# The second layout of an inner weight made by a transpose of the updated first one, and a gate's bias added by VectorE instead of by products

## What is computed

```python
def _recon(params, z):
    W1, b1, W2, b2 = params
    h = jax.nn.gelu(z @ W1.T + b1, approximate=False)
    return z + h @ W2.T + b2
def step(params, x):
    z, y = x @ t_k.T, x @ t_v.T
    grads = jax.grad(loss_fn)(params, z, y)      # mean squared error of _recon(params, z) against y
    new_params = tree_map(lambda p, g: p - LR * g, params, grads)
    return new_params, _recon(new_params, x @ t_q.T)
_, outs = jax.lax.scan(step, (W1, b1, W2, b2), in_seq)
```

```python
h2 = _rmsnorm(x, ffn_norm_w)
glogits = h2 @ gate_w + gate_b                   # 32 experts
topv, topi = jax.lax.top_k(glogits, 4)
gw = jax.nn.softmax(topv)
y2 = sum over the chosen experts e of gw_e * ((silu(g) * u) @ W_down[e]),  u, g = halves of h2 @ W_up[e]
```

## Time and profile before

| | |
|---|---|
| median of 3 runs | 968.82 us (968.16 to 969.98) |
| profiled execution | 970.77 us, of which the span of the core's instructions is 968.7 us |
| TensorE matmul busy | 849.8 us (88%), weight loads 649.2 us (67%) |
| VectorE, ScalarE, GpSimd busy | 762.2 us (79%), 593.1 us (61%), 478.4 us (49%) |
| mean granted TensorE clock | 0.943 of full |
| `layers` | to about 740 us; `experts` from there to the end |

### The profile page before, as it was taken

How to read it: one execution, slowest core, us unless ns; L and a number is a source line. 1 busy time by engine, 2 the same in 40 slices (tenths; PEclk the granted TensorE clock), 3 DMA queues, 4 the chain that set the end, 5 groups by cost and what they waited for, 6 DMA issues and landing times. The chain is left out here.

```text
span 968.7 us, 21670 instructions
## 1 busy us (share of the span) xinstructions
PE 849.8 (88%) x6666; PEld 649.2 (67%) x6666; DVE 762.2 (79%) x2734; ACT 593.1 (61%) x1900; POOL 478.4 (49%) x609
## 2 busy tenths in 40 slices
PE   1788999999999999999999999999984699999700
PEld 0445677777777777777777777777762588888600
DVE  2647979889898898989989898888865477777618
ACT  0114877768777786877868777687771366564300
POOL 1213223545555455555455555457436267777740
PEclk7699999999999999999999999999996799999955
DMA  6879999999940000000000000000001454444149
GB/s 160 261 241 374 375 374 375 370 371 366 364 109 20 8 19 17 11 21 11 19 10 17 18 14 20 7 19 26 19 16 39 110 142 125 132 128 112 53 134 334
DMA packets 97346, 129.41 MB, mean 134 GB/s; under 512 B 14513, under 2 KB 54354, under 8 KB 97234
## 3 DMA queue, kind: packets, MB, share of 16 engines
q1 hardware_dynamic: 84690, 108.36, 33.9%
q0 software_dynamic: 8192, 17.58, 5.5%
q10 hardware_dynamic: 4352, 2.10, 0.7%
HBM read 30.34 MB, written 97.65 MB: 132 GB/s over the span
## 5 line engine op out<-in xcount | busy, mean ns | idle before, releaser
L1322 POOL TENSOR_TENSOR l_t_cos<-l_t_cos,l_t_sin 128x512 f32<-128x512 f32 (+1 forms) x96 | 114.7, 1194 | 232.6 <-DVE l_t_sin L908 232.4
L1157 ACT ACTIVATE l_prob<-l_score,l_nm 128x128 f32<-128x128 f32 (+1 forms) x512 | 212.4, 437 | 19.6 <-DVE l_nm L767 19.3
L1543 POOL DMA_INDIRECT expert_out<-e_yo,e_dest x128 | 122.7, 958 | 59.6 <-issue 32.9
L94 POOL DMA_INDIRECT expert_rows<-h,slot x128 | 129.6, 1012 | 40.3 <-issue 34.0
L1167 ACT COPY l_probT<-l_turned 128x512 f32<-128x512 f32 x192 | 111.4, 593 | 59.0 <-PE l_turned L391 57.1
L756 DVE TENSOR_REDUCE l_mx<-l_score 128x2 f32<-128x512 f32 (+1 forms) x192 | 123.4, 684 | 23.2 <-PE l_score L377 22.0
L391 PEld LDWEIGHTS l_turned<-ident_sb,l_prob 128*128 128x128 f32 x768 | 87.6, 141 | 49.3 <-issue 41.2
L1157 ACT ACTIVATION_READ_ACCUMULATOR l_prob<-l_score,l_nm 128x1 f32 x512 | 113.1, 221 | 0.0
L391 PE MATMUL l_turned<-ident_sb,l_prob 128*128 128x128 f32 x768 | 111.1, 278 | 1.3 <-DVE l_prob L741 0.6
L377 PE MATMUL l_score<-l_kT,l_qT 64*128 64x128 f32 (+1 forms) x1024 | 109.8, 343 | 0.0
L406 PE MATMUL l_turned<-l_probT,l_vv 128*64 128x128 f32 x1536 | 105.1, 279 | 1.3 <-ACT l_probT L1167 1.3
(11 more groups left out here) (270 smaller groups left out, 1729.0 us busy)
## 6 DMA issues: line engine op xcount, KB each, us to landing
expert_rows<-zeros SPq DMA_DIRECT2D x32, 2240.0 KB, 22.5
e_xt<-expert_rows SPq DMA_DIRECT2D x160, 70.0 KB
e_yo<-expert_out SPq DMA_DIRECT2D x16, 512.0 KB, 5.9
wup_sb<-in_wup SPq DMA_DIRECT2D x1, 4096.0 KB, 15.2
expert_rows<-zeros SPq DMA_DIRECT2D x32, 70.0 KB, 2.1
expert_rows<-zeros SPq DMA_DIRECT2D x4, 560.0 KB, 12.2
expert_rows<-h,slot POOLq DMA_INDIRECT x128, 2.4
expert_out<-e_yo,e_dest POOLq DMA_INDIRECT x128
```

The costliest lines, as they stand in the source:

```text
L94: m["nc"].gpsimd.indirect_dma_start(m["xs"], bass.IndirectOffsetOnAxis(ap=m["slot"][:, par, c:c + 1], axis=0), m["h2"][:, par, c // TOPK, ...
L1157: ins = A_.activation(prob[:, b, h, cols], score[(2 * u + h) % 3][:, cols], ACT.Exp, bias=nm[:, b, h, j:j + 1], scale=0.125, accum_out=sum ...
L1322: g.tensor_tensor(t_cos[:, c % 2, 0:w], t_cos[:, c % 2, 0:w], t_sin[:, c % 2, 0:w], ALU.add).then_inc(s["added"], 1)
L1543: g_.indirect_dma_start(m["ys"], bass.IndirectOffsetOnAxis(ap=dest[:, t:t + 1], axis=0), yo[:, t, :], None).then_inc(sent[t % GROUP], 16)
```

## The change

W2's gradient in its first layout (L512) is no longer made. `update` writes only `fast[:, 0]` in its first instruction, and from the second sequence on W2 is made from `fast2` by a transpose on TensorE at the head of `residual_cols`, which ScalarE copies to `fast[:, 1]` right behind `rT`; `residual_rows`, which writes to the same columns of the bank, waits for this copy (`w2`). The gate's bias is summed over its three parts once, in n = 1, and kept in SBUF as `gate_b`; the two products L355 of the gate are gone, and VectorE adds `gate_b` where it copied.

```diff
+        gate_b = sb("gate_b", [P, EXPERTS])
@@ residual_cols, TensorE
                 pe.wait_ge(s["a_tok"], F + 1)
                 pe.wait_ge(s["z"], F + 1)
+                if F > 0:
+                    tr(side_f[:, TOK:TOK + P], fast2[:], ident[:])
                 mm(side_f[:, 0:TOK], dkvT[:], xnT[:, par, :], start=True, stop=False)
@@ residual_rows, TensorE
                 pe.wait_ge(s["rT"], F + 1)
+                after(pe, s["w2"], F)
@@ gradients, TensorE
-                for t in range(TPS):
-                    mm(side_f[:, HID:2 * HID], r[:, t, :], h[:, t, 0:HID], start=(t == 0), stop=(t == TPS - 1))
@@ gate, TensorE
-                    bias(side_g[:, cols], QKV + D, QKV + D + EXPERTS)
-                    ins = mm(side_g[:, cols], h2T[:, t * P:(t + 1) * P], m["gate"][:], start=False, stop=True)
+                    ins = mm(side_g[:, cols], h2T[:, t * P:(t + 1) * P], m["gate"][:], start=True, stop=True)
@@ idle, TensorE, n = 1
+                    mm(turned[1][:, 0:EXPERTS], m["ones_bf"][:], m["bias3"][:, QKV + D:QKV + D + EXPERTS],
+                       start=True, stop=True).then_inc(s["fold_ps"], 1)
@@ update, VectorE
-                V.scalar_tensor_tensor(out=fast[:, :, 0:HID], in0=side_f[:, 0:2 * HID].rearrange("p (a k) -> p a k", a=2),
-                                       scalar=GRAD_SCALE, in1=fast[:, :, 0:HID],
+                V.scalar_tensor_tensor(out=fast[:, 0, 0:HID], in0=side_f[:, 0:HID], scalar=GRAD_SCALE, in1=fast[:, 0, 0:HID],
@@ pick, VectorE
-                V.tensor_copy(glog[:], side_g[:, 0:TPS * EXPERTS].rearrange("p (t e) -> p t e", t=TPS)) \
-                    .then_inc(s["glog"], 1)
+                if B == 0:
+                    v.wait_ge(s["folded"], 5)
+                V.tensor_tensor(glog[:], side_g[:, 0:TPS * EXPERTS].rearrange("p (t e) -> p t e", t=TPS),
+                                gate_b[:, None, :].broadcast_to([P, TPS, EXPERTS]), ALU.add).then_inc(s["glog"], 1)
@@ first_stats, VectorE, n = 1
+                    if u == 10:
+                        v.wait_ge(s["fold_ps"], 4)
+                        V.tensor_copy(gate_b[:], turned[1][:, 0:EXPERTS]).then_inc(s["folded"], 1)
@@ rT_out, ScalarE
                 A_.copy(rT[:], side_f[:, 0:TOK]).then_inc(s["rT"], 1)
+                if n > 0:
+                    A_.copy(fast[:, 1, 0:HID], side_f[:, TOK:TOK + HID]).then_inc(s["w2"], 1)
```

More of the change, by code:

```diff
@@ L285, in layers @@
         names = (
-            "folded fold_ps filled cleared part constants bias_in ready stat0 rs0 xn xT_ps xT z_ps zT a_ps aT az_ps a_tok z expo gelu tanh slope apdf sloped "
+            "w2 folded fold_ps filled cleared part constants bias_in ready stat0 rs0 xn xT_ps xT z_ps zT a_ps aT az_ps a_tok z expo gelu tanh slope apdf sloped "
             "rT_ps rT hr_ps h r dh_ps da g_ps w out_ps x1 "
```

## The result

The median of the changed kernel is 962.48 us (960.90 to 962.75, 4 runs) beside 968.69 us for the kernel before on the same chip (968.16 to 969.98, 4 runs): ratio 0.9925, 95% interval 0.9913 to 0.9938. The direction and the main mechanism came out, the size did not. In the profiled executions the span fell by 8.1 us, from 968.7 to 960.6.

The account below looks back on a forecast made before the run. TensorE's full stream, then VectorE's chain, was taken as the bound. Terms summed to -4.57 us (964.25), or -6.27 (962.55) without the wait; the middle was 963.4 us, bounds 962.0 to 965.2, range with rivals 962.0 to 969.2.

Parts of the forecast that it names:

- the group of gradients: On TensorE, removing L512 was to save 0.44 us an iteration, 0.37 at the lower end.
- the transpose: On TensorE, the new float32 transpose was to cost 0.22 us an iteration, bounds 0 and 0.39.
- the gate: On TensorE, dropping both bias products was to save 0.09 us an iteration, between 0.06 and 0.13.
- ScalarE's copy: Between `rT` and L1167's copy on ScalarE: 0 to 0.17 us could reach the scores, taken as 0.
- `xn`'s wait: At ten boundaries, n = 5 to 14: TensorE regains 0.17 us each if L790 loses its stall, -1.7 us.
- The sign that I had named: On VectorE, time between starts of L881 in successive iterations falls by 0.3 to 0.5 us if the forecast is right.
- What bounds the kernel: TensorE's matmuls cover 24.00 of 24 us; VectorE, busy 23.33, passes gains on only through its chain behind the gradients.
- n = 3, n = 16 to 19: Iterations outside the full pattern: n = 3 without a gate -0.22 us; n = 16 to 19, only gate products, -0.36.
- n = 0 and n = 1: The fill: n = 0 without L512 saves 0.57 us; n = 1 pays 0.30 for transpose and `gate_b` product.
- ScalarE and the new wait: TensorE's wait in `residual_rows` for the copy is covered by work between; without cover it costs the copy's 0.24 us.
- Rival 1: At VectorE's chain: GpSimd pins L790, so `x_turn` starts where it did; 967.65 us, chance 0.31.
- Rivals 2 and 3: ScalarE's queue makes it slower, 971.8 us, chance 0.09; TensorE saves less than the instructions say, 966.7 us, chance 0.12.

Follow-up runs that it names:

- experiment 4: Kernel before with the gradient and update of the second weight's first layout left out, no transpose or copy: 962.26 us, ratio 0.9907.
- experiment 3: Changed kernel with its transpose of the second weight done three times instead of once: 965.30 us, ratio 0.9937.
- experiment 1: Kernel before with only the second layout made by transpose and copy, the gate as before: 963.27 us, ratio 0.9922.
- experiments 4 and 9: Kernel before without the first layout's gradient, 962.26 us; kernel before with GpSimd's product ahead of its last pair of transfers, 968.38 us.
- experiment 2: Kernel before with only the gate's part, its bias products replaced by VectorE's add: 970.33 us, ratio 0.9993.
- experiment 10: Changed kernel run again unaltered beside the kernel before, in more rounds: 962.94 us, ratio 0.9932.
- Experiment 7: Changed kernel with two more copies on ScalarE ahead of the new one, three in all: 965.22 us, ratio 0.9943.
- experiment 9: Kernel before with GpSimd's product moved ahead of its last pair of transfers: 968.38 us, ratio 0.9986.
- experiment 6: Changed kernel with one of the two products of the removed gradient group put back: 966.59 us, ratio 0.9952.
- experiment 11: Changed kernel with TensorE's operands in transposes and two gradient groups cut to the part used: 969.50 us, ratio 0.9995.

## Why the prediction was off, point by point

The iteration as the runs decompose it, in us:

| | forecast, n = 4 to 15 | measured | from |
|---|---|---|---|
| the group of gradients | -0.44 | -0.45 | experiment 4, n = 4 and 5 |
| the transpose | +0.22 | +0.11 | experiment 3 |
| the gate | -0.09 | -0.06 | after against experiment 1 |
| ScalarE's copy | 0 | 0 | experiments 1, 3, 4 |
| sum without the wait | -0.31 | -0.40 | after, n = 4 and 5: -0.41, -0.39 |
| `xn`'s wait, from n = 6 | -0.17, half of it taken | -0.21 | experiments 4 and 9 |

-0.45 + 0.11 - 0.06 - 0.21 = -0.61, which is what the change shows. Over the twelve: 12 x (-0.40) - 10 x 0.21 = -6.9, and the trace has 6.89. The forecast had -3.72, and with half of the wait -4.57. The sign that I had named, a fall of 0.3 to 0.5 us from one update to the next, was passed by 0.1.

- **What bounds the kernel.** Right: with TensorE's stream full, what is taken from it comes through, and the second limit is VectorE's chain behind the gradients.
- **The transpose: the step that failed.** I read the row "x2" of the earlier trace rows as the two records of one float32 transpose. A float32 product does show two matmuls, but a transpose shows one, and the row holds the transposes of two tiles. The row of the changed kernel has x1 and 0.11 us. The mistake was worth 0.11 x 12 = 1.3 us. The same row gave 0.11 for each record, and I had even written that down, as 0.11 for each of "the two records"; what I missed was the count, and the loop over two tiles in the code would have told it.
- **The wait of `xn`: mechanism right, size too small.** I said that `xn` would start with the transfer, not in its midst, and so lose its stall. It starts 0.07 ahead of it and takes 0.59. By taking the middle between "stays" and "goes" as the forecast I described a case that no run shows: in each kernel the wait is there at all ten boundaries or gone at all ten. I also sized it by the idle time ahead of the load, 0.17 (0.16 to 0.19 at the ten boundaries), where it is worth 0.21: behind the wait the first record of `x_turn` holds the next start back for 0.14 us instead of 0.11, which is the rest. Together 10 x 0.21 - 0.85 = 1.25 us.
- **The gate.** 0.06, the lower end that I had named, not 0.09. Alone it gives 0.02 or nothing from n = 6 on (experiment 2), which I had not said.
- **n = 3, n = 16 to 19.** Forecast -0.22 and -0.36, measured +0.07 (37.41 to 37.48; 37.45 in the other execution) and 0.00 from the last update to the end. In n = 3 TensorE stands idle for 2.4 us before the change, waiting for GpSimd's additions and for ScalarE, and for 2.8 us after it (in experiment 10's execution): what was taken from it became idle time. I had priced these stages as if they were full. At the end, +0.33 in the other execution, the -0.36 can't be told from scatter.
- **n = 0 and n = 1.** Forecast -0.57 and +0.30, in the profiled executions -0.74 and +0.15. Both lie within the scatter of this stretch, so neither price is tested. In the changed kernel VectorE's wait in n = 0 shrank from 1.00 to 0.29 us, as the step said.
- **ScalarE and the new wait.** Right for the single copy in the full iterations. Experiment 7 shows that three are too many. In n = 1, where the cover that I had counted on is not there, the new wait does hold TensorE: `residual_rows` (L479) stands 0.21 us for the copy, in both executions of the changed kernel, and its load starts 0.58 us behind `rT` instead of 0.43. I had named the copy's 0.24 as the price without cover, but my account of n = 1 had none of it.
- **Rival 1** did not come for the whole change, but it is what happens to the gate's part alone. Its reading of n = 4 was not exact: there the product ends at 166.28 and the first `xn` right behind it, at 166.36, while the second follows freely to 166.62. **Rivals 2 and 3** did not come. The Trainium skill's rule that I weighed with rival 1 ("SBUF — State Buffer", section Who interferes with whom: whoever starts first holds the shared ports for the whole instruction) fits the product: in experiment 9 the first `xn` meets it after 0.04 us and the pair takes 1.02 instead of 0.59. It does not fit the transfer from its start on: in experiment 2 the first `xn` began 0.23 us inside one and took its usual 0.34 (the second took 1.33, until the product behind the transfer was over).
- **The range.** Its lower end was 962.0. With the transpose at its lower bound of 0 and the wait gone in full my own bounds gave about 959.5 (an estimate from the same terms); the range did not follow the bounds down.

The gap between the 8.1 us of the profiled executions and the 6.2 us of the medians is that of two executions: the profiled one of the kernel before took 970.77 us, 1.95 more than the median of the others. 0.69 us of it is x, which came later in that one; that the rest is the filling, which scatters by 1 to 2 us between executions of one kernel, is likely but not shown, since the other executions left no trace.

## What to carry to other kernels

Count what a row's "x" stands for before using its duration: match it with the loops of the code, for products and transposes separately. When two engines take turns on something, a stall may be there in full or not at all, as in all runs here, so forecast one of the two and give the other a chance of its own; and look at which instruction of the third engine is under way, since a change of order there may buy the same gain (0.22 us of 0.61 here, with one line moved). Price an instruction only in the stages in which its engine is full. Before a little idle time of TensorE is called slack, count its records against the loads beside them.

## What the runs showed of the hardware

How long the two `xn` take depends on where they start against GpSimd's indirect transfer of 0.96 us and the product behind it, with the same instructions each time. Starts are differences of two records, durations those of the first and the second instruction:

| start of `xn` behind the start of the transfer | first, second, us | kernel |
|---|---|---|
| -0.06 to -0.17 | 0.34, 0.34 | the change, both executions |
| +0.04 | 0.34, 0.87 | three transposes, n = 11 |
| +0.12 | 0.33, 0.78 | half of the group put back |
| +0.23 | 0.34, 1.33 | the gate's part alone |
| +0.27 to +0.30 | 0.88, 0.74 | before |

A shift of 0.04 us between the last two moves the delay from the second instruction to the first. The rows sort by where each of the two starts in the transfer (the second starts 0.26 behind an undelayed first): up to 0.23 us behind its start it is not held; at 0.27 to 0.38 it ends 1.15 to 1.17 behind the transfer's start, about 0.2 behind its end; from 0.49 on it ends 0.1 behind the product's end. So it is a later part of the transfer that holds VectorE, not the whole of it. The earlier transfer, of 1.10 us, shows the same on `hn`: an instruction that starts up to 0.42 us behind its start takes 0.34; one that starts 0.49 to 0.75 behind mostly ends 1.11 to 1.12 behind, with the transfer's end, and so takes up to 0.62; from 0.77 on it takes 0.34 again, which ends no sooner. That `hn` lost nothing in the kernel before, 0.85 inside the transfer, was its place there; my prediction had used it as evidence about the transfer without asking for the place.

The times grow on the other side in turn. GpSimd's product takes 0.75 before and 1.21 to 1.26 in the changed kernel, where VectorE's `prob` starts ahead of it and takes 0.99 to 1.11 instead of 0.69; where `prob` starts 0.3 behind the product (experiment 6), the product keeps its 0.75 and only `prob` takes 0.99.

A transpose of 32 or 33 partitions between products of 128 costs more than one of 128 (experiment 11): five of them in an iteration made it 0.54 us longer, by the steps into and out of the narrow shape. Of the four products with 32 or 33 weight columns beside them, the two with 33 took no less than full ones; the two with 32 took half, and the step ahead of them cost 0.2 us.
